# Routed expert layer with W1 as the stationary operand, fetched tile by tile

## The chip, the cores and the metric

One core of a Trainium2 chip runs the whole program. The metric is device microseconds of that core, median of several runs. The engines are PE (TensorE: matrix products, with PEld for its weight loads), DVE (VectorE), ACT (ScalarE), POOL (GpSimd) and SP (SyncE, which here only issues DMAs). A name with a q behind it, such as PEldq or SPq, is the sequencer of that engine. All data is float32.

## The reference, cut to what matters

The program applies four residual layers to 4096 tokens of width 256: linear attention, a routed expert layer, a state-space layer with a scan, and the expert layer once more with the same weights. Only the expert layer is touched:

```
logits = tokens @ Wr + br                    # tokens = layernorm(x), 4096 x 256, 8 experts
expert = argmax(softmax(logits)); max_prob = its probability
h = relu(tokens @ W1[expert] + b1[expert])   # W1: 8 x 256 x 512
y = h @ W2[expert] + b2[expert]              # W2: 8 x 512 x 256
x = x + y * max_prob
```

Each token goes through one expert only.

## The kernel before

The program is one `build` function with a section per engine; each engine executes its list in order, and semaphores (`wait_ge`, `then_inc`) join them. `feed(r)` is the expert layer, run for r = 0 (first stage below) and r = 1 (second stage). It normalises the rows, computes the logits, sorts tokens by expert and lays them into 39 tiles of 128 rows, each of one expert (`TILES = 39`). `tile_e` holds each tile's expert number, `idx` the row numbers. The semaphore `f_pos` says that `tile_e` is there, `f_idx` that `idx` is.

POOL gathers the rows of tile j into `t_x[j % 8]`, scatters the finished tile `t_y` to DRAM, and gathers tile j + 8. Even tiles use one set of buffers and PSUM banks, odd tiles the other (`par`). For each tile:

1. DVE `norm` (L917) writes the normalised rows `t_n`.
2. PE `tr` transposes them (2 transposes, L1108), ACT `xt` (L528) copies the result to `t_xt`.
3. PE `first` (L1261): the tokens are stationary, W1 of the tile's expert is moving, 512 columns wide; the result in `ps[2 + par]` has tokens on partitions.
4. DVE `hid` (L908) copies that to `t_h`.
5. PE `turn_hidden` transposes `t_h` in four 128 x 128 pieces (L1108) into `ps[4 + par]`.
6. ACT `relu` (L535, four instructions) adds b1, applies relu and writes `t_ht`.
7. PE `second` (L1278): `t_ht` is stationary, W2 is moving, 256 columns wide.
8. DVE `bias` (L927) and `result` (L934) make `t_y`.

A float32 product is executed as two passes, so `first` appears in the profile as 4 matmuls of 512 columns, `second` as 8 of 256 columns, and a transpose as one. All eight experts' W1 and W2 are in SBUF before a stage begins (`load_ffn`, 16 transfers of 512 KB and b2). PE reads the expert number from `tile_e` into a register (`expert`, L1253: a TENSOR_LOAD and some register instructions) right ahead of every `first` and every `second`. PE's order over a pair of tiles stands in the loop `turn`: turn_hidden(2i), first(2i+1), tr(2i+2), second(2i), turn_hidden(2i+1), first(2i+2), tr(2i+3), second(2i+1).

Of the kernel before, what the change touches and what calls it, by code (L numbers as in the profile page):

```python
# [17 lines left out]
P = 128  # L18
# [4 lines left out]
KD = D // P  # L23
# [63 lines left out]
AT_BANKS = ((6, 0, 3), (7, 3, 3), (1, 6, 2))  # L87


RING = 4  # L90


def h_buffers():
# [32 lines left out]
def build(nc, T):  # L126
    with ExitStack() as ctx:
# [52 lines left out]


        fs = Space(0)
        w1 = fs.take(E * KD * HID).rearrange("p (e k h) -> p e k h", e=E, k=KD)
        w2 = fs.take(E * KH * D).rearrange("p (e k d) -> p e k d", e=E, k=KH)
        b2 = fs.take(E * D).rearrange("p (e d) -> p e d", e=E)
        FEED = fs.at
# [41 lines left out]
        t_n = [s.take(D) for _ in range(2)]  # L228
        t_xt = [s.take(KD * P).rearrange("p (k t) -> p k t", k=KD) for _ in range(2)]
        assert s.at <= router + 4 * NCH * E, s.at  # L230
        s = Space(AR - 2 * KI * DI - KI * D - 5 * HID)
        t_h = [s.take(HID) for _ in range(2)]
        t_ht = [s.take(HID).rearrange("p (k t) -> p k t", k=KH) for _ in range(2)]
        t_y = [s.take(D) for _ in range(2)]
        s = Space(AR - 2 * KI * DI - KI * D)
# [49 lines left out]

        def load_ffn(eng, r):
            for e in range(E):
                eng.dma_start(w1[:, e], T["W1"][e].rearrange("(k p) h -> p k h", p=P)).then_inc(S(f"ld_ffn{r}"), 16)
                eng.dma_start(w2[:, e], T["W2"][e].rearrange("(k p) d -> p k d", p=P)).then_inc(S(f"ld_ffn{r}"), 16)
            eng.dma_start(b2, T["b2"].partition_broadcast(P)).then_inc(S(f"ld_ffn{r}"), 16)  # L290

        LD_FFN = 16 * (2 * E + 1)


        @block.sync
        def _(sp):
            xin = T["x"].rearrange("b (c p) d -> p b c d", p=P)
            for b in range(BATCH):
                if b == 1:
                    sp.dma_start(cst[:, :], T["cst"]).then_inc(S("ld_cst"), 16)  # L300
                sp.dma_start(x[:, b * CPB:(b + 1) * CPB, :], xin[:, b]).then_inc(S(f"ld_x{min(b, 1)}"), 16)
            sp.wait_ge(S("ld_x1"), 16 * (BATCH - 1))
            load_ffn(sp, 0)


            def store_rows(r, b):
                at = kept(b) if r else b * CPB
                sp.dma_start(xs[r][b * SEQ:(b + 1) * SEQ].rearrange("(c p) d -> p c d", p=P),
                             x[:, at:at + CPB, :]).then_inc(S(f"f{r}_rows"), 16)

            for b in range(BATCH):
                sp.wait_ge(S("a_xupd"), b + 1)
                store_rows(0, b)
            sp.wait_ge(S("row_zeroed"), 32)
            sp.dma_start(ipw, T["ip_x"].rearrange("(k p) d -> p k d", p=P)).then_inc(S("ld_ipw"), 16)
            for k in range(TAPS):
                if k >= 2:
                    sp.wait_ge(S("tap_mm"), KD * (k - 1))
                sp.dma_start(cw[k % 2], T["conv"][k].rearrange("(k p) d -> p k d", p=P)).then_inc(S(f"ld_cw{k}"), 16)

            sp.wait_ge(S("f0_st0"), 16 * (TURNS + 1))
            sp.wait_ge(S("f0_st1"), 16 * TURNS)
            for b in range(BATCH):
                sp.dma_start(x[:, b * CPB:(b + 1) * CPB, :],
                             x_mid[b * SEQ:(b + 1) * SEQ].rearrange("(c p) d -> p c d", p=P))\
                    .then_inc(S(f"ld_mid{min(b, 1)}"), 16)
            for b in range(BATCH):
                sp.wait_ge(S("m_bchi"), b + 1)
                sp.dma_start(c_rows[b % 2], m_bc[NS:2 * NS, :]).then_inc(S("m_cst"), 16)
                sp.wait_ge(S("m_cst"), 16 * (b + 1))  # L330
                for n in range(NS):
                    i = NS * b + n
                    if i >= RC:
                        sp.wait_ge(S("m_cp"), i - RC + 1)
                    if n == NS - 4 and b:
                        sp.wait_ge(S("m_xupd"), 2 * b)
                        store_rows(1, b - 1)
                    if n == 2 and 2 <= b < BATCH - 2:
                        new = b + RING - 2
                        sp.wait_ge(S("f1_rows"), 16 * (b - 1))  # L340
                        if b > 2:
                            sp.wait_ge(S("ld_again"), 16 * (b - 2))
                        sp.dma_start(x[:, kept(new):kept(new) + CPB, :],
                                     x_mid[new * SEQ:(new + 1) * SEQ].rearrange("(c p) d -> p c d", p=P))\
                            .then_inc(S("ld_again"), 16)
                    sp.dma_start(m_c[i % RC], c_rows[b % 2][n].partition_broadcast(P)).then_inc(S(f"m_cl{i % RC}"), 16)
            sp.wait_ge(S("m_y"), KI * BATCH)
            sp.wait_ge(S("f1_rows"), 16 * (BATCH - 1))
            sp.dma_start(x[:, RING * CPB:, :], xs[1][0:RING * SEQ].rearrange("(c p) d -> p c d", p=P))\
                .then_inc(S("ld_back"), 16)  # L350
            sp.wait_ge(S("m_xupd"), 2 * BATCH)
            store_rows(1, BATCH - 1)
            load_ffn(sp, 1)
            sp.wait_ge(S("f1_st0"), 16 * (TURNS + 1))
            sp.wait_ge(S("f1_st1"), 16 * TURNS)

# [81 lines left out]
        def _(a):  # L438
# [66 lines left out]
            def feed(r):  # L505
# [18 lines left out]

                def xt(par, n):
                    a.wait_ge(S(f"f{r}_tr{par}"), n + 1)
                    a.wait_ge(S(f"f{r}_h{par}"), n)
                    a.activation(t_xt[par], ps[par][:, 0:KD * P].rearrange("p (k t) -> p k t", k=KD), ACT.Copy)\  # L528
                        .then_inc(S(f"f{r}_xt{par}"), 1)

# [13 lines left out]
                a.wait_ge(S("f_pos"), r + 1)  # L544
                xt(0, 0)
                xt(1, 0)

                def turn(i, more):
                    relu(expert(2 * i), 0, i)
                    xt(0, i + 1)  # L550
                    relu(expert(2 * i + 1), 1, i)
                    if more:
                        xt(1, i + 1)

                turn(0, True)
                with a.Fori(1, H - 1) as i:
                    turn(i, True)
                turn(H - 1, False)
                relu(expert(TILES - 1), 0, H)

            feed(0)
            for k in range(TAPS // 2, TAPS):
# [113 lines left out]
        def _(v):  # L676
# [144 lines left out]
            def feed(r, updated, n_updated):  # L821
# [80 lines left out]
                v.tensor_copy(idx, r_col).then_inc(S("f_idx"), 1)  # L902
                link(v.tensor_copy(tabs, ps[4][:, 0:NV * COLS].rearrange("p (v j) -> p v j", v=NV)))

                def hid(par, n):
                    v.wait_ge(S(f"f{r}_h{par}"), n + 1)
                    v.wait_ge(S(f"f{r}_ht{par}"), n)
                    v.tensor_copy(t_h[par], ps[2 + par][:, :]).then_inc(S(f"f{r}_hc{par}"), 1)  # L908

                def norm(k, par):  # L910

                    j = 2 * k + par
# [24 lines left out]
                v.wait_ge(S(f"ld_ffn{r}"), LD_FFN)  # L937
                norm(0, 0)
                norm(0, 1)
                hid(0, 0)  # L940
                for k in range(TURNS):
                    norm(k + 1, 0)
                    hid(1, k)
                    bias(k, 0)
                    if k < TURNS - 1:
                        norm(k + 1, 1)
                    result(k, 0)
                    hid(0, k + 1)
                    bias(k, 1)
                    result(k, 1)  # L950
                bias(TURNS, 0)
# [153 lines left out]
        def _(t):  # L1105
# [104 lines left out]
            def feed(r):  # L1210
# [43 lines left out]
                                        min_val=0, max_val=E - 1)  # L1254

                def first(j, par, n):
                    e = expert(j)
                    t.wait_ge(S(f"f{r}_xt{par}"), n + 1)
                    t.wait_ge(S(f"f{r}_hc{par}"), n)
                    for k in range(KD):  # L1260
                        last = t.matmul(ps[2 + par][:, :], t_xt[par][:, k, :],  # L1261
                                        w1[:, row(e), k, :].rearrange("p a h -> p (a h)"),
                                        start=(k == 0), stop=(k == KD - 1))
                    last.then_inc(S(f"f{r}_h{par}"), 1)

                def turn_hidden(par, n):
                    t.wait_ge(S(f"f{r}_hc{par}"), n + 1)
                    t.wait_ge(S(f"f{r}_relu{par}"), n)
                    for k in range(KH):
                        last = turned(ps[4 + par][:, k * P:(k + 1) * P], t_h[par], k, 0)  # L1270
                    last.then_inc(S(f"f{r}_ht{par}"), 1)

                def second(j, par, n):
                    e = expert(j)
                    t.wait_ge(S(f"f{r}_relu{par}"), n + 1)
                    t.wait_ge(S(f"f{r}_y{par}"), n)
                    for k in range(KH):
# [9 lines left out]
                tr(1, 0)  # L1287
                first(0, 0, 0)

                def turn(i, more):  # L1290
                    turn_hidden(0, i)
                    first(2 * i + 1, 1, i)
                    tr(0, i + 1)
                    second(2 * i, 0, i)
                    turn_hidden(1, i)
                    first(2 * i + 2, 0, i + 1)
                    if more:
                        tr(1, i + 1)
                    second(2 * i + 1, 1, i)

                turn(0, True)
                with t.Fori(1, H - 1) as i:
                    turn(i, True)
                turn(H - 1, False)
                turn_hidden(0, H)
                second(TILES - 1, 0, H)

            def logits(r, b):
                t.wait_ge(S("f_xt"), BATCH * r + b + 1)
# [229 lines left out]
```

## Time and profile before

| | |
|---|---|
| median of 3 runs | 1665.94 us (1663.62 to 1668.23) |
| profiled execution | 1664.5 us, its span 1662.5 us |
| PE busy | 1431.1 us of the span |
| DVE, ACT, POOL busy | 1117.9, 951.9, 915.3 us |
| first expert stage, tiles 0 to 38 | about 293 to 466 us of the span |
| second expert stage, tiles 0 to 38 | about 1478 us to the end |

The busy shares are means over stages of different kinds; this change touches the two expert stages, some 350 us together. The span is 2.0 us shorter than the time of the same execution, and that time is 1.4 us under the median.

### The profile page before, as it was taken

The page shows a single profiled execution, that of the slowest core. Times are in us where ns is not written, and L with a number is a line of the kernel's source. Part 1 is how long each engine was busy: PE and PEld are TensorE (multiplying, and loading weights), DVE is VectorE, ACT ScalarE, POOL GpSimd, SP SyncE. Part 2 cuts the span into 40 slices and gives each one's busy share as a digit, 9 for nine tenths or more (in the row PEclk, how much of TensorE's full clock was granted, in tenths as well). Part 3 has the DMA queues.
Part 4 walks back from the last instruction along what each step waited for, and adds up shares of the span by engine and source line. Part 5 has one row for each costly group of instructions (what it writes and reads, how often), then busy time and mean ns, then how long its engine had stood idle before and what let it go on. Part 6 is the DMA issues. An engine that isn't in the chain of part 4 may idle for free.

```text
span 1662.5 us, 21266 instructions
## 1 busy us (share of the span) xinstructions
PE 1431.1 (86%) x6310; PEld 929.5 (56%) x6311; DVE 1117.9 (67%) x1703; ACT 951.9 (57%) x1749; POOL 915.3 (55%) x417
## 2 busy tenths in 40 slices
PE   2899877999998898989989999999996635779997
PEld 1566575566643555555655556555564524746664
DVE  5566546344451689999889998889999954354443
ACT  1222211333322899898998989999898840113332
POOL 1111000444300499979989898998989981024442
PEclk9999968999999899999999999999997875579999
DMA  9300021111130296894958949589494985211120
GB/s 311 131 25 25 26 76 54 58 61 59 44 102 14 50 221 138 186 202 114 219 129 200 215 115 219 132 194 212 108 220 111 211 182 198 92 30 60 59 60 17
DMA packets 81314, 202.87 MB, mean 122 GB/s; under 512 B 9609, under 2 KB 40462, under 8 KB 68688
## 3 DMA queue, kind: packets, MB, share of 16 engines
q0 software_dynamic: 21376, 119.30, 33.4%
q1 hardware_dynamic: 55632, 78.91, 14.9%
q10 hardware_dynamic: 4224, 3.67, 0.7%
q8 instruction: 38, 0.62, 0.1%
q14 instruction: 44, 0.36, 0.1%
HBM read 84.14 MB, written 18.88 MB: 62 GB/s over the span
## 4 chain that ended last, share of the span: by engine, by line
PE 63%; DVE 12%; ACT 10%; issue 8%; POOL 4%; DMA 2%; SPq 1%; ACTq 1%; POOLq 0%; DVEq 0%
PE ps L1108 13%; PE ps L1344 10%; PE ps L1278 9%; PE ps L1261 8%; DVE arena L1056 4%; PE ps L1373 4%; ACT arena L620 4%; ACT arena L630 3%; PE ps L1133 3%; PE ps L1313 3%; POOL arena L413 2%; PE ps L1415 2%; PE ps L1170 2%; PE ps L1124 2%; PE ps L1206 2%
## 5 line engine op out<-in xcount | busy, mean ns | idle before, releaser
L1108 PEld LDWEIGHTS ps<-cst,arena 128*128 128x128 f32 x2836 | 373.7, 151 | 407.6 <-issue 255.2
L1108 PE MATMUL ps<-cst,arena 128*128 128x128 f32 x2836 | 458.5, 291 | 113.4 <-ACT arena L630 48.4
L413 POOL TENSOR_TENSOR arena<-arena 128x2048 f32<-128x2048 f32 x98 | 460.3, 4699 | 119.0 <-DVE arena L1056 91.5
L1056 DVE TENSOR_TENSOR_SCAN arena<-arena,ps 128x512 f32<-128x512 f32 x392 | 471.2, 1212 | 62.1 <-PE ps L1108 54.6
L620 ACT ACTIVATE arena<-arena,a_neg 128x512 f32<-128x512 f32 x512 | 366.4, 716 | 50.7 <-DVE arena L1056 39.5
L630 ACT ACTIVATE arena<-arena,m_bt 128x512 f32<-128x512 f32 x512 | 363.3, 710 | 1.1 <-PE ps L1108 1.1
L1344 PE MATMUL ps<-arena,tapw 128*128 128x512 f32 x512 | 260.4, 608 | 0.0
L382 POOL DMA_INDIRECT arena<-rows,arena x78 | 75.7, 970 | 250.0 <-DVE arena L902 226.5
L535 ACT ACTIVATE arena<-ps,b1t 128x128 f32<-128x128 f32 x312 | 89.0, 368 | 168.5 <-PE ps L1108 110.2
L1278 PE MATMUL ps<-arena 128*128 x624 | 151.3, 385 | 6.6 <-ACT arena L535 3.2
L1056 DVE TENSOR_TENSOR_SCAN x<-arena,ps 128x512 f32<-128x512 f32 x120 | 143.9, 1211 | 18.6 <-PE ps L1108 16.5
L1261 PE MATMUL ps<-arena 128*128 x312 | 152.4, 612 | 0.8 <-issue 0.8
L413 POOL TENSOR_TENSOR x<-x,arena 128x2048 f32<-128x2048 f32 x30 | 140.1, 4670 | 5.7 <-DMA arena<-c_rows 4.2
L1373 PE MATMUL ps<-arena,dtw 128*128 128x512 f32 x256 | 130.7, 598 | 2.2 <-ACT arena L585 1.2
L1278 PEld LDWEIGHTS ps<-arena 128*128 128x128 f32 x624 | 112.3, 190 | 28.6 <-issue 16.5
L927 DVE TENSOR_TENSOR arena<-ps,arena 128x256 f32<-128x256 f32 x78 | 33.2, 425 | 123.3 <-PE ps L1278 71.0
L1415 PE MATMUL ps<-outw,arena 128*128 128x256 f32 x256 | 74.3, 407 | 37.6 <-DVE arena L1016 37.6
L908 DVE COPY arena<-ps 128x512 f32<-128x512 f32 x78 | 54.0, 692 | 78.2 <-PE ps L1261 78.2
L1344 PEld LDWEIGHTS ps<-arena,tapw 128*128 128x128 f32 x512 | 85.0, 195 | 29.5 <-issue 28.4
L373 POOL TENSOR_TENSOR x<-x,arena 128x1024 f32 (+1 forms) x8 | 18.8, 2350 | 132.0 <-DVE arena L711 126.7
L396 POOL DMA_INDIRECT out_x<-arena x39 | 39.5, 1013 | 92.1 <-DVE arena L934 92.1
L528 ACT ACTIVATE arena<-ps 128x256 f32<-128x256 f32 x78 | 29.9, 384 | 104.5 <-PE ps L1108 87.1
(152 smaller groups left out, 1668.6 us busy)
## 6 DMA issues: line engine op xcount, KB each, us to landing
arena<-arena POOLq DMA_DIRECT2D x45, 1024.0 KB, 8.8
arena<-c_rows SPq DMA_DIRECT2D x128, 256.0 KB, 3.8
x<-arena POOLq DMA_DIRECT2D x29, 1024.0 KB, 8.4
arena<-in_W SPq DMA_DIRECT2D x32, 512.0 KB, 10.2
arena<-x POOLq DMA_DIRECT2D x15, 1024.0 KB, 9.0
rows<-x SPq DMA_DIRECT2D x16, 512.0 KB, 3.3
x<-x POOLq DMA_DIRECT2D x7, 1024.0 KB, 8.9
x<-residual SPq DMA_DIRECT2D x12, 512.0 KB, 5.5
```

The source lines that it names most:

```text
L382: g.indirect_dma_start(out=t_x[j % XB], out_offset=None, in_=xs[r], in_offset=bass.IndirectOffsetOnAxis(ap=idx[:, j:j + 1], axis=0))\
L413: g.tensor_tensor(h, h, m_c[i % RC].unsqueeze(1).to_broadcast([P, KI, SEQ]), ALU.mult)\
L535: last = a.activation(t_ht[par][:, k, :], ps[4 + par][:, k * P:(k + 1) * P], ACT.Relu, bias=b1t[:, row(e), k:k + 1].rearrange("p a b -> p ...
L620: a.activation(m_a[g % RA], m_dt[b % 2][:, k, :], ACT.Exp, scale=a_neg[:, k, n:n + 1])\
L630: a.activation(m_dbt[i % 2][:, c, :], m_wt[b % 2][:, c, :], ACT.Copy, bias=1e-6, scale=m_bt[b % 2][:, c, n:n + 1]).then_inc(S("m_dbt"), 1)
L1056: v.tensor_tensor_scan(out=h[:, k, :], data0=m_a[g % RA], data1=ps[SCAN_BANK[g % 3]][:, :], initial=0.0, op0=ALU.mult, op1=ALU.add).then_i ...
L1108: return t.transpose(bank, src[:, k * P:(k + 1) * P], ident)
L1261: last = t.matmul(ps[2 + par][:, :], t_xt[par][:, k, :], w1[:, row(e), k, :].rearrange("p a h -> p (a h)"), start=(k == 0), stop=(k == KD ...
L1278: last = t.matmul(ps[6 + par][:, 0:D], t_ht[par][:, k, :], w2[:, row(e), k, :].rearrange("p a h -> p (a h)"), start=(k == 0), stop=(k == K ...
L1344: mm = t.matmul(ps[CONV_BANK[o]][:, :], tapw[:, k, d, o * P:(o + 1) * P], m_xt[n % 2][:, d, k:k + SEQ], start=(i == 0), stop=(i == TAPS * ...
L1373: mm = t.matmul(ps[DT_BANK[o]][:, :], dtw[:, k, o * P:(o + 1) * P], m_u[n % 2][:, k, :], start=(k == 0), stop=(k == KI - 1))
L1415: mm = t.matmul(ps[OUT_BANK[h]][:, (c % 2) * D:(c % 2) * D + D], m_sz[:, k, c * P:(c + 1) * P], outw[:, k, :], start=(k == 0), stop=(k == ...
```

## The change

W1 becomes the stationary operand of the first product. For each quarter h of the 512 hidden units, the product of W1's 128 x 128 block and the transposed tokens gives the hidden layer already transposed, in `ps[4 + par]`. So `hid` on DVE and `turn_hidden` on PE go, with their buffers. A tile's W1 (512 KB) is no longer resident: SP reads the tile's expert number, waits until the buffer's last reader, tile j - 4, is through its first product, and issues one DMA into `t_w1[j % 4]`. PE's `first` needs no register then, gets a wait for its W1 buffer and one for the relu of the tile that used its PSUM bank before; `second` gets its expert number from a read placed ahead of the `first` before it. PE's loop is written out. ACT's `relu` of an even tile stands at the end of a turn instead of the start of the next, which keeps ACT's order of work the same.

```diff
-RING = 4
+RING, WR = 4, 4
...
-        w1 = fs.take(E * KD * HID).rearrange("p (e k h) -> p e k h", e=E, k=KD)
+        t_w1 = [fs.take(KD * HID).rearrange("p (k h) -> p k h", k=KD) for _ in range(WR)]
...
             for e in range(E):
-                eng.dma_start(w1[:, e], T["W1"][e].rearrange("(k p) h -> p k h", p=P)).then_inc(S(f"ld_ffn{r}"), 16)
                 eng.dma_start(w2[:, e], T["W2"][e].rearrange("(k p) d -> p k d", p=P)).then_inc(S(f"ld_ffn{r}"), 16)
...
+            def send_w1(r):
+
+                sp.wait_ge(S("f_pos"), r + 1)
+                for j in range(TILES):
+                    if j >= WR:
+                        sp.wait_ge(S(f"f{r}_ht{j % 2}"), (j - WR) // 2 + 1)
+                    e = sp.value_load(tile_e[0:1, j:j + 1], min_val=0, max_val=E - 1)
+                    sp.dma_start(t_w1[j % WR], T["W1"][ds(e, 1)].rearrange("a (k p) h -> p (a k) h", p=P))\
+                        .then_inc(S(f"f{r}_w{j % WR}"), 16)
...
-                def hid(par, n):
-                    v.wait_ge(S(f"f{r}_h{par}"), n + 1)
-                    v.wait_ge(S(f"f{r}_ht{par}"), n)
-                    v.tensor_copy(t_h[par], ps[2 + par][:, :]).then_inc(S(f"f{r}_hc{par}"), 1)
...
                 def first(j, par, n):
-                    e = expert(j)
+
                     t.wait_ge(S(f"f{r}_xt{par}"), n + 1)
-                    t.wait_ge(S(f"f{r}_hc{par}"), n)
-                    for k in range(KD):
-                        last = t.matmul(ps[2 + par][:, :], t_xt[par][:, k, :],
-                                        w1[:, row(e), k, :].rearrange("p a h -> p (a h)"),
-                                        start=(k == 0), stop=(k == KD - 1))
-                    last.then_inc(S(f"f{r}_h{par}"), 1)
-
-                def turn_hidden(par, n):
-                    t.wait_ge(S(f"f{r}_hc{par}"), n + 1)
                     t.wait_ge(S(f"f{r}_relu{par}"), n)
-                    for k in range(KH):
-                        last = turned(ps[4 + par][:, k * P:(k + 1) * P], t_h[par], k, 0)
+                    t.wait_ge(S(f"f{r}_w{j % WR}"), 16 * (j // WR + 1))
+                    for h in range(KH):
+                        for k in range(KD):
+                            last = t.matmul(ps[4 + par][:, h * P:(h + 1) * P], t_w1[j % WR][:, k, h * P:(h + 1) * P],
+                                            t_xt[par][:, k, :], start=(k == 0), stop=(k == KD - 1))
                     last.then_inc(S(f"f{r}_ht{par}"), 1)
...
-                def turn(i, more):
-                    turn_hidden(0, i)
+                for i in range(H):
+                    even = expert(2 * i)
                     first(2 * i + 1, 1, i)
                     tr(0, i + 1)
-                    second(2 * i, 0, i)
-                    turn_hidden(1, i)
+                    second(even, 0, i)
+                    odd = expert(2 * i + 1)
                     first(2 * i + 2, 0, i + 1)
-                    if more:
+                    if i < H - 1:
                         tr(1, i + 1)
-                    second(2 * i + 1, 1, i)
...
-                turn_hidden(0, H)
-                second(TILES - 1, 0, H)
+                second(expert(TILES - 1), 0, H)
```

This is PE's order before, inside the loop of the first stage, for one even tile: the hidden turn, the first product of the next tile, the token turn, and the second product (L1108 is either kind of transpose, ISA a register instruction).

```order
L1108 MATMUL ps<-cst,arena 128x128 [waits f0_relu0,f0_hc0]
L1108 MATMUL ps<-cst,arena 128x128 x3
L1253 ISA
L1253 TENSOR_LOAD tile_e
L1253 ISA x2
L1261 ISA [waits f0_hc1,f0_xt1]
L1261 MATMUL ps<-arena 128x512
L1261 ISA
L1261 MATMUL ps<-arena 128x512
L1245 REGISTER_ALU
L1108 MATMUL ps<-cst,arena 128x128 [waits f0_xt0,f0_n0]
L1108 MATMUL ps<-cst,arena 128x128
```

Behind these stood a second TENSOR_LOAD and the second product. Now the same place reads as follows, with L1265 the first product, L1110 the token turn and L1274 the second product.

```order
L1255 TENSOR_LOAD tile_e
L1255 ISA x2
L1265 MATMUL ps<-arena 128x128 [waits f0_w3,f0_relu1,f0_xt1]
L1265 MATMUL ps<-arena 128x128 x7
L1110 MATMUL ps<-cst,arena 128x128 [waits f0_xt0,f0_n0]
L1110 MATMUL ps<-cst,arena 128x128
L1274 ISA [waits f0_y0,f0_relu0]
L1274 MATMUL ps<-arena 128x256
```

The four hidden transposes are gone, eight narrow products stand for two wide ones, one register read is left, and nothing but the second product's own register instructions stands between the token turn and it.

SP had nothing to do during the tiles: its queue went from the tap weights straight to the residual, as here.

```order
L319 DMA arena<-in_conv 128x4x512 [waits tap_mm] x2
L324 DMA x<-residual 128x4x256 [waits f0_st1,f0_st0]
L324 DMA x<-residual 128x4x256 x7
L329 DMA c_rows<-arena 16x512 [waits m_bchi]
L346 DMA arena<-c_rows 128x512 [waits m_cst]
```

Between the first two of these rows now stand 39 groups of the kind shown next; this is SP's queue around the fifth tile.

```order
L316 DMA arena<-in_W 128x2x512
L315 TENSOR_LOAD tile_e [waits f0_ht0]
L315 ISA x2
L316 ISA
L316 DMA arena<-in_W 128x2x512
```

From the fifth tile on, each transfer of W1 is released by the first product four tiles back.

## Rows read from the trace of the kernel before

**Rows 1.** Window, first expert stage: PE, PEld, DVE, ACT, POOL, clock, DMA, GB/s
```profile
303.00:453.00 150.00, 148.33 (x634) 100.15 (x633) 65.83 (x140) 53.37 (x175) 65.58 (x66) 1.00 0.18 54
```

**Rows 2.** Chain, one tile of the second stage: start, duration, work
```profile
1499.43 0.44 PE ps L1108 x4
1499.87 1.72 PE ps L1261 x4
1501.81 1.73 PE ps L1278 x8
```

**Rows 3.** Chain, both ends of the second stage
```profile
1475.60 2.73 DMA arena<-rows,arena
...
1479.68 3.79 PE ps L1261 x4
1483.50 0.70 DVE arena L908
...
1489.15 1.73 PE ps L1278 x8
...
1647.23 1.73 PE ps L1278 x8
...
1650.83 2.00 PE ps L1278 x8
```

**Rows 4.** Chain, both ends of the first stage
```profile
294.23 3.64 PE ps L1261 x4
...
301.71 1.73 PE ps L1278 x8
...
459.65 1.73 PE ps L1278 x8
...
463.54 1.99 PE ps L1278 x8
```

**Rows 5.** Timeline of PE's weight loads around one token turn
```profile
1496.55 0.14 PEld L1108 LDWEIGHTS ps<-cst,arena 128*128 128x128 f32 x1 [0.24 <-DVE arena L917]
...
1497.44 1.59 PEld L1278 LDWEIGHTS ps<-arena 128*128 128x128 f32 x8 [0.32 <-issue]
```

**Rows 6.** Timeline of PE, the row behind the second product ahead of that turn
```profile
1494.82 0.60 PE L1108 MATMUL ps<-cst,arena 128*128 128x128 f32 x4
```

**Rows 7.** Timeline of DVE in the same stretch
```profile
1495.14 0.42 DVE L927 TENSOR_TENSOR arena<-ps,arena 128x256 f32<-128x256 f32 x1 [1.38 <-PE ps L1278]
...
1496.01 0.41 DVE L917 TENSOR_SCALAR arena<-arena 128x256 f32<-128x256 f32 x1
```

**Rows 8.** Line L1253, PE's read of the expert number: ns min/median/max
```profile
L1253 PEldq TENSOR_LOAD <-tile_e x156: 296/302/495, 293.2 to 1648.0; - x156
```

**Rows 9.** Chain in the attention stage: eight transposes, sixteen passes of 129 columns
```profile
152.30 0.87 PE ps L1108 x8
153.17 1.79 PE ps L1154 x16
```

**Rows 10.** Chain in the logits: sixteen passes of 8 columns
```profile
229.63 3.21 PE ps L1313 x16
```

**Rows 11.** Window over the logits; the third last number is the granted clock
```profile
228.00:256.00 28.00, 28.00 (x136) 28.00 (x134) 4.14 (x12) 5.43 (x10) 0.00 (x0) 0.50 0.00 1
```

**Rows 12.** Timeline of ACT, one relu of a tile
```profile
1495.55 1.15 ACT L535 ACTIVATE arena<-ps,b1t 128x128 f32<-128x128 f32 x4 [1.88 <-issue]
```

**Rows 13.** Timeline of POOL: scatter of one tile, gather of another
```profile
1496.94 1.02 POOL L396 DMA_INDIRECT out_x<-arena  x1 [1.56 <-DVE arena L934]
1498.26 0.97 POOL L382 DMA_INDIRECT arena<-rows,arena  x1 [0.30 <-issue]
```

**Rows 14.** DMA issues, 1384 to 1415 us: KB each, median us to landing
```profile
arena<-in_W SPq DMA_DIRECT2D x16, 512.0 KB, 9.9
...
rows<-x SPq DMA_DIRECT2D x1, 512.0 KB, 3.3
```

**Rows 15.** Timeline of DVE where tile_e is written, second stage
```profile
1471.41 0.18 DVE L899 TENSOR_SCALAR tile_e<-arena 128x40 int32<-128x40 f32 x1
```

More of the change, by code:

```diff
@@ L230, in build @@
         assert s.at <= router + 4 * NCH * E, s.at
-        s = Space(AR - 2 * KI * DI - KI * D - 5 * HID)
-        t_h = [s.take(HID) for _ in range(2)]
+        s = Space(AR - 2 * KI * DI - KI * D - 3 * HID)
         t_ht = [s.take(HID).rearrange("p (k t) -> p k t", k=KH) for _ in range(2)]
@@ L287, in load_ffn @@
             for e in range(E):
-                eng.dma_start(w1[:, e], T["W1"][e].rearrange("(k p) h -> p k h", p=P)).then_inc(S(f"ld_ffn{r}"), 16)
                 eng.dma_start(w2[:, e], T["W2"][e].rearrange("(k p) d -> p k d", p=P)).then_inc(S(f"ld_ffn{r}"), 16)
             eng.dma_start(b2, T["b2"].partition_broadcast(P)).then_inc(S(f"ld_ffn{r}"), 16)
-        LD_FFN = 16 * (2 * E + 1)
+        LD_FFN = 16 * (E + 1)
         @block.sync
@@ L319, in _ @@
                 sp.dma_start(cw[k % 2], T["conv"][k].rearrange("(k p) d -> p k d", p=P)).then_inc(S(f"ld_cw{k}"), 16)
+            send_w1(0)
             sp.wait_ge(S("f0_st0"), 16 * (TURNS + 1))
@@ L353, in _ @@
             load_ffn(sp, 1)
+            send_w1(1)
             sp.wait_ge(S("f1_st0"), 16 * (TURNS + 1))
@@ L526, in xt @@
                     a.wait_ge(S(f"f{r}_tr{par}"), n + 1)
-                    a.wait_ge(S(f"f{r}_h{par}"), n)
+                    a.wait_ge(S(f"f{r}_ht{par}"), n)
                     a.activation(t_xt[par], ps[par][:, 0:KD * P].rearrange("p (k t) -> p k t", k=KD), ACT.Copy)\
@@ L546, in feed @@
                 xt(1, 0)
+                relu(expert(0), 0, 0)
                 def turn(i, more):
-                    relu(expert(2 * i), 0, i)
                     xt(0, i + 1)
@@ L553, in turn @@
                         xt(1, i + 1)
+                    relu(expert(2 * i + 2), 0, i + 1)
                 turn(0, True)
@@ L558, in feed @@
                 turn(H - 1, False)
-                relu(expert(TILES - 1), 0, H)
             feed(0)
@@ L939, in feed @@
                 norm(0, 1)
-                hid(0, 0)
                 for k in range(TURNS):
                     norm(k + 1, 0)
-                    hid(1, k)
                     bias(k, 0)
@@ L947, in feed @@
                     result(k, 0)
-                    hid(0, k + 1)
                     bias(k, 1)
@@ L1256, in first, with second @@
                 def first(j, par, n):
-                    e = expert(j)
                     t.wait_ge(S(f"f{r}_xt{par}"), n + 1)
-                    t.wait_ge(S(f"f{r}_hc{par}"), n)
-                    for k in range(KD):
-                        last = t.matmul(ps[2 + par][:, :], t_xt[par][:, k, :],
-                                        w1[:, row(e), k, :].rearrange("p a h -> p (a h)"),
-                                        start=(k == 0), stop=(k == KD - 1))
-                    last.then_inc(S(f"f{r}_h{par}"), 1)
-                def turn_hidden(par, n):
-                    t.wait_ge(S(f"f{r}_hc{par}"), n + 1)
-                    t.wait_ge(S(f"f{r}_relu{par}"), n)
-                    for k in range(KH):
-                        last = turned(ps[4 + par][:, k * P:(k + 1) * P], t_h[par], k, 0)
+                    t.wait_ge(S(f"f{r}_relu{par}"), n)
+                    t.wait_ge(S(f"f{r}_w{j % WR}"), 16 * (j // WR + 1))
[3 more added lines that the diff above has]
+                                            t_xt[par][:, k, :], start=(k == 0), stop=(k == KD - 1))
                     last.then_inc(S(f"f{r}_ht{par}"), 1)
-                def second(j, par, n):
-                    e = expert(j)
+                def second(e, par, n):
                     t.wait_ge(S(f"f{r}_relu{par}"), n + 1)
@@ L1288, in feed @@
                 first(0, 0, 0)
-                def turn(i, more):
-                    turn_hidden(0, i)
+                for i in range(H):
+                    even = expert(2 * i)
                     first(2 * i + 1, 1, i)
                     tr(0, i + 1)
-                    second(2 * i, 0, i)
-                    turn_hidden(1, i)
+                    second(even, 0, i)
+                    odd = expert(2 * i + 1)
                     first(2 * i + 2, 0, i + 1)
-                    if more:
+                    if i < H - 1:
                         tr(1, i + 1)
-                    second(2 * i + 1, 1, i)
[L1301 to L1304, printed above, removed]
-                turn_hidden(0, H)
-                second(TILES - 1, 0, H)
+                    second(odd, 1, i)
+                second(expert(TILES - 1), 0, H)
             def logits(r, b):
```

## The prediction

> **What bounds the kernel now.** I read three views for the two expert stages: windows, the chain, then the timelines. In a window of 150 us inside the first stage PE is busy for 148 us at the full granted clock, while DVE, ACT and POOL have 66, 53 and 66 us of work [rows 1]. So PE's own list sets the pace there. The chain agrees, in both stages alike: a tile is a hidden turn of 0.44 us, a first product of 1.72 and a second of 1.73, all PE [rows 2]; the token turn, half a hidden turn, is 0.22. These make 4.11 us. From the second product of tile 0 to that of tile 37, 37 tiles on, the second stage takes 1647.23 - 1489.15 = 158.08 us, or 4.27 a tile [rows 3], and the first 157.94, the same 4.27 [rows 4]. The missing 0.16 is in one place of each pair of tiles. DVE ends a norm at 1496.01 + 0.41 = 1496.42 [rows 7], the token turn's load is released by it, and the loads of the second product start only at 1497.44, after 0.32 us without work [rows 5]. In that 1.02 us PE's sequencer, which had stood at the norm's semaphore, reads the expert number (0.30 us for the TENSOR_LOAD alone [rows 8]) and works out addresses. Everywhere else the read is hidden, because the sequencer runs ahead of the array.
>
> **The steady tile after the change.** Removed: the hidden turn, 0.44 us of PE, and DVE's copy. DVE is not the bound, so the copy counts only where it stood in the way of something.
>
> Exchanged: 4 passes of 512 columns for 16 passes of 128. The columns are the same, 2048, but there are 16 weight loads of 128 x 128 instead of 4, so what matters is whether a load fits behind 128 moving columns. The nearest row is the key/value product of the attention stage, a stationary 128 x 128 from SBUF with 129 columns moving: 16 passes in 1.79 us, and 8 transposes in 0.87 [rows 9]. These give 1.78 and 1.74 us for 16 passes. The load alone is seen where almost nothing moves: 16 passes of 8 columns take 3.21 us, 0.20 each [rows 10], but at half the clock [rows 11], so 0.10 at the full one, against 0.107 for the columns. It fits, barely. I take 1.75 for the first product, 0.03 more than now.
>
> A rule speaks against this. The Trainium skill, "TensorE: Matmul & The Clock Gate", section "Back-to-back issue gap", says that in a real stream the spacing is set by the load and the product together, about 81 ns at 128 columns where the product alone would need 56. By that ratio, as an estimate from the page, the first product would take about 2.5 us and the kernel would lose. The row of 129 columns in float32 does not show such an addition, and the sum goes by the row.
>
> Moved: the register read. It now stands ahead of the first product, where the sequencer is some 1.2 us ahead of the array (it has passed a second product of 1.73 us within about half a microsecond, at one register instruction per product). The read and its register work cost about 0.65 of that, my estimate: the 1.02 us less what the semaphore, the turn's dispatch and the first load need. So the gap of 1.02 us behind a norm shrinks to about 0.35, nearly covered by the turn itself. This returns most of the 0.16 a tile.
>
> New on the same place: the norm is late next. The second product ahead of a norm hands over at 1494.82 [rows 6]; DVE's bias, result and norm follow and end at 1496.42 [rows 7], 1.60 us later, with no copy between them in the old order either. PE needs 0.05 us to see it and 0.1 for the load, so the turn can start at 1.75. Before, a hidden turn and a first product (2.16) covered this; now a first product of 1.75 alone does. I expect a wait of 0 to 0.3 us per pair of tiles, for the norms of even tiles only (the other norm stands ahead of the result in DVE's list), and take 0.15, the middle.
>
> A tile: 1.75 + 0.22 + 1.73 + 0.075 = 3.775 us. Against 4.27 that is 0.495 less; times 37, 18.3 a stage, 36.6 in both.
>
> **The other engines at this pace.** ACT must bring the relu between the end of a first product and the second product of the same tile, which are a first product and a turn of other tiles apart, 1.97 us, plus a second product. It takes 1.15 [rows 12], some 0.3 to hear of PE, and the wait for the copy ahead of it: free by over a microsecond. POOL needs from a result to the end of the next gather 0.9 to start (from DVE's next operation at 1496.01 [rows 7] to 1496.94), 1.02, 0.30 and 0.97, together 3.2 us [rows 13], less than 3.775 by 0.6. SP, idle until now, waits, reads and issues once a tile, about 1.2 us by my estimate, 0.65 for the read and half a microsecond for the issue. Behind its waits stand only later W1 transfers and, after the last, the load of the residual, which waits for the last scatter anyway.
>
> W1's transfer: a buffer is freed at the end of a first product and needed four tiles on, 4 x 3.775 - 1.75 = 13.3 us later. SP takes 1.2 of these; a 512 KB transfer lands 3.3 us after issue alone and 9.9 in a queue of seventeen [rows 14]. In this stage at most one or two are in flight, 0.5 MB in 3.775 us beside 55 GB/s of rows [rows 1], so I take 4 to 6 us. Cost 0; it starts to cost above 12 us. The transfers of a dynamic address on SP are not in the trace; below, a static issue bounds them, above, the queue of seventeen.
>
> **The ends of a stage.** Start: from the first product of tile 0 to the second product of tile 0 the second stage took 9.47 us [rows 3], the first 7.48 [rows 4], at half the clock for most of it; in it stand a copy of 0.70 us on DVE [rows 3] and a hidden turn, 0.88 at half the clock, with nothing else for PE to do. These go. The clock may rise later relative to the work, since the work comes sooner. I take 1.5 a stage (bounds 0.5 and 2.8). Against it stands that the first four W1 transfers, 2 MB, now run beside the first gathers, of which the first takes 2.73 us to land and is on the chain [rows 3]. `tile_e` is written at 1471.6 [rows 15], 8 us ahead of the first product, so W1 of tile 0 is there in time; the gathers may land later. I take 0.5 a stage (0 to 2).
>
> End: from the end of tile 37's second product to the start of tile 38's passed 1650.83 - 1648.96 = 1.87 us in the second stage and 463.54 - 461.38 = 2.16 in the first [rows 3, 4], for a hidden turn and a relu that nothing covered. Now tile 38's relu runs beside the second product of tile 37. Gain 4.0 together.
>
> Less W1 in `load_ffn` frees 4 MB of early transfers; the work that follows them waits for other things, so 0.
>
> **Sum.** 36.6 + 3.0 - 1.0 + 4.0 = 42.6 us. From the profiled execution's 1664.5, 1621.9; it was 1.4 under the median of the runs, so 1622 to 1623. I say 1622.
>
> **Rivals.**
> *The load shows.* If half of each 0.10 us load stood outside the columns, the first product would take 16 x 0.157 = 2.5 us, a tile 4.53, and the kernel 74 x 0.26 - 6 = 13 us more: 1679. With the whole load outside, 16 x 0.207 = 3.3, a tile 5.3, 1739. It decides from 0.145 us a pass on. The page named above says something like the first. Against it: 0.111 a pass measured [rows 9]. Chance 3 in 100.
> *The clock falls.* In the logits PE is busy throughout, with passes of 8 columns and transposes, and is granted half the clock [rows 11]. If that came with the new stage's passes too, a tile would take 3.7 us more, and 11 such tiles of 78 would use up the gain. Against it: the logits move 8 columns where these move 128 and 256, the array is filled as before, and transposes are fewer. Chance 2; a fourth of the tiles so: 1694.
> *W1 comes late.* Should a transfer need over 15.6 us from a free buffer to landing, a tile takes over (15.6 + 1.75) / 4 = 4.35 us and the kernel is slower; at 18 us, 4.9 a tile, 1709. Only a queue of seventeen came near that. Chance 2.
> *A partial wait.* W1's traffic or the tighter round of DVE and POOL costs something on every tile, through late norms, gathers or scatters, and the tile takes 3.9 to 4.1: 74 x 0.27 + 6 = 26 us gained at 4.0, 1640. POOL's slack of 0.6 and the norm's of nothing speak for it. Chance 13.
> *It does nothing,* because the sequencer can't cover the read and the waits with 16 loads to issue: PE stays at 4.27. Chance 2.
> *The forecast,* 78. Its own range: tiles of 3.70 to 3.87 (43 or 30 us), ends between 10 and 3 us, so 1613 to 1633.
>
> **Numbers.** The range reaches into the partial wait: 1612 to 1636. A difference under 0.3% (5 us) can't be told from none. Faster: forecast, partial wait and a bit, 92; same 2; slower 6.
>
> **What would show it.** Right: 16 passes at L1265 in 1.75 us, no gap over 0.1 us behind the token turn, 3.7 to 3.8 us between second products, SP's W1 landing within 6 us, PE waiting nowhere for a W1 semaphore, the clock at 1.00. Wrong: loads of L1265 that leave gaps, a token turn that waits for DVE L917 by more than 0.3 us per pair, PE idle released by a DMA into arena, late first gathers, a clock under 1 between tiles 3 and 38.

## The result, and the profile after

| | before | after |
|---|---|---|
| median of 4 runs | 1664.78 us (1663.61 to 1668.23) | 1615.16 us (1611.79 to 1626.81) |
| ratio after / before | | 0.9722, interval 0.9695 to 0.9749 |
| span of the profiled execution | 1662.5 us | 1615.4 us |

The profiled execution of the changed kernel took 1617.17 us, 2.0 over the median. PE's share and the groups that answer to the changed lines, from the page of the changed kernel:

```profile
PE 1385.1 (86%) x6934; PEld 979.2 (61%) x6934; DVE 1063.7 (66%) x1625; ACT 952.1 (59%) x1749; POOL 916.6 (57%) x417
L1265 PE MATMUL ps<-arena 128*128 128x128 f32 x1248 | 155.8, 280 | 0.0
L1274 PE MATMUL ps<-arena 128*128 x624 | 147.4, 380 | 0.0
```

A window inside each stage (busy us of PE, PEld, DVE, ACT, POOL; clock; DMA share; GB/s), to be held against [rows 1]:

```profile
303.00:433.00 130.00, 130.00 (x908) 122.75 (x907) 41.60 (x105) 53.01 (x174) 65.23 (x66) 1.00 0.66 197
1470.00:1590.00 120.00, 120.00 (x839) 113.40 (x838) 38.54 (x98) 48.94 (x161) 62.60 (x63) 1.00 0.68 208
```

PE has no idle time left at the full clock; the DMA engines now carry 200 GB/s instead of 54, and DVE has 42 us of work in 130. The chain, for one tile and both ends of the first stage, answers to [rows 2] and [rows 4]:

```profile
283.92 5.13 DMA arena<-rows,arena
289.74 0.66 PE ps L1110 x2
290.40 1.53 issue
291.93 0.69 PE ps L1110 x2
292.62 5.20 PE ps L1265 x32
298.03 1.73 PE ps L1274 x8
299.76 1.78 PE ps L1265 x16
301.55 0.22 PE ps L1110 x2
301.76 1.73 PE ps L1274 x8
...
436.08 3.57 PE ps L1274 x16
439.64 13.78 PE ps L1208 x32
```

A tile is 1.78 + 0.22 + 1.73 = 3.73 us with no gap. The second products of tiles 37 and 38 stand as one piece of 16 passes at 436.08: the wait of 2.16 us at the end of the stage is gone. The second stage, also from the chain:

```profile
1448.89 5.11 DMA arena<-rows,arena
...
1455.35 2.04 issue
1457.39 0.69 PE ps L1110 x2
1458.07 6.11 PE ps L1265 x32
...
1464.40 1.73 PE ps L1274 x8
...
1602.26 1.74 PE ps L1274 x8
```

At both starts the gather of tile 0 takes 5.1 us to land. What PE waits for last is the gather of tile 1, for both token turns stand ahead of the first product in PE's list. The 2.73 us of [rows 3] is that gather too: POOL issues it behind the gather of tile 0. These are its issue and the norm that it releases, in the first stage of the changed kernel:

```profile
285.27 0.97 POOL L392 DMA_INDIRECT arena<-rows,arena  x1 [0.30 <-issue]
291.40 0.47 DVE L922 TENSOR_SCALAR arena<-arena 128x256 f32<-128x256 f32 x1 [1.81 <-DMA arena<-rows,arena]
```

From issue to norm pass 6.13 us, and 6.66 in the second stage; before it was 2.76 in both. The token turn of tile 1 so comes 2.2 and 2.7 us behind that of tile 0.

Split by pieces of the two spans:

| piece | before | after | difference |
|---|---|---|---|
| 37 tiles, first stage | 157.94 | 138.05 | -19.9 |
| 37 tiles, second stage | 158.08 | 137.86 | -20.2 |
| from tile 37's second product to PE's next work (L1208) | 5.88 | 3.56 | -2.3 |
| the same to the end of the span, second stage | 15.27 | 13.14 | -2.1 |
| start of each stage, from the cast of `idx` to the second product of tile 0 | 14.02, 15.77 | 15.00, 16.35 | +1.0, +0.6 |
| everything else (attention, logits, sort, scan) | | | -4.1 |

The last line can't be laid to the change. Of it, 2.8 us are in the first logits, which are the same code. From the first to the last record of the logits product passed 33.45 and 36.56 us in the two stages of the kernel before, 30.62 and 36.55 after. The granted clock was 1.00 for the first 3.4 us of the 33.45 and for the first 6.5 us of the 30.62, then 0.50; in both stretches of 36.6 it was 0.50 from the start. In all profiles of this study, of whichever kernel, the stretch is near one of 30.6, 33.5 and 36.6. Another 1.4 us are ahead of the first logits, which begin at 222.5 us before and 221.1 after; in the thirteen profiles they begin between 218.3 and 222.7, with no order by kernel.

### The profile page after: what moved, and what is told of

It reads as the page before. It is cut to its first block, busy times and chain, and to the rows that moved or that the text cites. A ratio compares the mean times of both kernels' runs of the same rounds, so it can differ in the third digit from the quotient of the medians.

```text
span 1615.4 us, 22069 instructions
## 1 busy us (share of the span) xinstructions
PE 1385.1 (86%) x6934; PEld 979.2 (61%) x6934; DVE 1063.7 (66%) x1625; ACT 952.1 (59%) x1749; POOL 916.6 (57%) x417
## 4 chain that ended last, share of the span: by engine, by line
PE 62%; ACT 11%; DVE 11%; issue 8%; POOL 4%; DMA 2%; SPq 1%; ACTq 1%; POOLq 0%; DVEq 0%
PE ps L1110 11%; PE ps L1334 10%; PE ps L1265 9%; PE ps L1274 8%; ACT arena L630 4%; ACT arena L640 4%; PE ps L1363 4%; DVE arena L1058 4%; PE ps L1135 3%; PE ps L1303 3%; POOL arena L423 2%; PE ps L1405 2%; PE ps L1172 2%; PE ps L1126 2%; PE ps L1208 2%
## 5 line engine op out<-in xcount | busy, mean ns | idle before, releaser
L1110 PEld LDWEIGHTS ps<-cst,arena 128*128 128x128 f32 x2524 | 330.8, 152 | 364.0 <-issue 234.2
L1110 PE MATMUL ps<-cst,arena 128*128 128x128 f32 x2524 | 410.2, 293 | 119.4 <-ACT arena L640 49.3
L392 POOL DMA_INDIRECT arena<-rows,arena x78 | 76.0, 974 | 246.0 <-DVE arena L912 222.5
L1265 PEld LDWEIGHTS ps<-arena 128*128 128x128 f32 x1248 | 155.6, 197 | 3.8
L1265 PE MATMUL ps<-arena 128*128 128x128 f32 x1248 | 155.8, 280 | 0.0
L1274 PE MATMUL ps<-arena 128*128 x624 | 147.4, 380 | 0.0
L1274 PEld LDWEIGHTS ps<-arena 128*128 128x128 f32 x624 | 112.5, 190 | 12.4 <-issue 0.2
L521 ACT ACTIVATE arena<-ps 128x512 f32<-128x512 f32 x32 | 17.4, 594 | 113.4 <-PE ps L1110 113.4
```

The lines of the kernel that those rows point to most:

```text
L392: g.indirect_dma_start(out=t_x[j % XB], out_offset=None, in_=xs[r], in_offset=bass.IndirectOffsetOnAxis(ap=idx[:, j:j + 1], axis=0))\
L1110: return t.transpose(bank, src[:, k * P:(k + 1) * P], ident)
L1265: last = t.matmul(ps[4 + par][:, h * P:(h + 1) * P], t_w1[j % WR][:, k, h * P:(h + 1) * P], t_xt[par][:, k, :], start=(k == 0), stop=(k == ...
L1274: last = t.matmul(ps[6 + par][:, 0:D], t_ht[par][:, k, :], w2[:, row(e), k, :].rearrange("p a h -> p (a h)"), start=(k == 0), stop=(k == K ...
```

## The experiments

In all of them "a tile" is the mean over 36 tiles, from the start of tile 0's second product to tile 36's, first and second stage, and "the start" is the stretch from the cast of `idx` to tile 0's second product. On this scale the kernel before has 4.277 and 4.281, the changed kernel 3.737 and 3.732. Ratios are to the kernel before as timed beside each experiment: its median was 1664.69 us beside the three on the read and the first hold, 1663.61 beside the later ones on the hold, and 1662.72 beside the others.

### The register read alone

```diff
-                def first(j, par, n):
-                    e = expert(j)
+                def first(e, par, n):
...
-                def second(j, par, n):
-                    e = expert(j)
+                def second(e, par, n):
...
+                    nums[1] = expert(2 * i + 1)
+                    first(nums[1], 1, i)
...
-                    second(2 * i, 0, i)
+                    second(nums[0], 0, i)
```

> The kernel before, with PE's register read alone changed: each tile's expert number is read once, ahead of its first product, and kept for its second. Theory (the read behind the norm's semaphore makes the gap of each pair): a tile falls from 4.27 to 4.11 to 4.14 us, the kernel by 10 to 12 us, to about 1654. Rival (the gap is the norm's lateness or the loop's branch, and the read hides anyway): 4.27 a tile, 1665.

Measured: 1649.33 us, ratio 0.9916 (0.9896 to 0.9935), a tile 4.103 in both stages. The timeline of PE's weight loads, as in [rows 5]:

```profile
384.71 0.14 PEld L1108 LDWEIGHTS ps<-cst,arena 128*128 128x128 f32 x1 [0.24 <-DVE arena L917]
385.14 0.14 PEld L1108 LDWEIGHTS ps<-cst,arena 128*128 128x128 f32 x1 [0.29 <-issue]
385.25 1.60 PEld L1276 LDWEIGHTS ps<-arena 128*128 128x128 f32 x8
```

The turn's first load is released by the norm as before, and the second product's loads now follow without idle time. 74 tiles by 0.176 is 13 us of the 15.4 between the medians; the rest was not followed up. This edit includes the written-out loop, so that was run by itself too:

```diff
-                turn(0, True)
-                with t.Fori(1, H - 1) as i:
-                    turn(i, True)
-                turn(H - 1, False)
+                for i in range(H):
+                    turn(i, i < H - 1)
```

> The kernel before with PE's loop over the tiles written out and nothing else. Theory: the branch stands where the sequencer is ahead, so 4.27 us a tile as before, 1663 to 1668. Rival: the branch or the reading of instructions costs something, and the tile changes by over 0.03 us.

Measured: 1659.67 us in one run, 4.219 and 4.255 a tile. So up to 0.06 of the 0.176 is the loop and not the place of the read; it is not quite nothing, as I had thought. In the first stage the chain still has 0.24 us of the gap per pair: every other second product takes 1.97 us there in place of 1.73. In a loop the number's address takes a register instruction ahead of the TENSOR_LOAD, on the same late path; that this is the cause was not tested apart.

### The read put back

```diff
-                    even = expert(2 * i)
                     first(2 * i + 1, 1, i)
                     tr(0, i + 1)
-                    second(even, 0, i)
-                    odd = expert(2 * i + 1)
+                    second(expert(2 * i), 0, i)
```

> The changed kernel with PE's read put back right ahead of the second product. Theory: at the turns of even tiles the sequencer stands at the norm's semaphore until 1.64 us after the second product before, then needs the 1.02 us of the kernel before up to the first load: 2.66 instead of 1.89, 0.77 us per pair, 0.39 a tile, so 4.11 us a tile and 28 us more, about 1643. Rival (the read hides once the hidden turn is gone): 3.73 a tile, 1615.

Measured: 1639.09 us, ratio 0.986 (0.9841 to 0.9879), a tile 4.093 and 4.097. The chain has the gap where it was foretold, behind one token turn of two:

```profile
381.74 1.78 PE ps L1265 x16
383.53 0.22 PE ps L1110 x2
383.75 0.35 issue
384.10 1.99 PE ps L1274 x8
386.09 1.78 PE ps L1265 x16
387.87 0.22 PE ps L1110 x2
```

The other turn, whose norm is early, has none. A pair is 0.72 us longer than in the changed kernel, of which the chain shows 0.35 as idle and 0.26 in the second product behind it, 1.99 in place of 1.73. So without the early read the change would have gained about half. The two parts don't add: the read costs 0.12 to 0.18 a tile in the kernel before and 0.36 here. The numbers fit the hidden turn having covered part of the norm's lateness: 0.35 a pair before, plus the 0.38 by which hidden turn and first product (2.16) were longer than the first product alone (1.78), gives 0.73. This was not tested by itself.

### W1 without the stream

```diff
-        t_w1 = [fs.take(KD * HID).rearrange("p (k h) -> p k h", k=KD) for _ in range(WR)]
+        w1 = fs.take(E * KD * HID).rearrange("p (e k h) -> p e k h", e=E, k=KD)
...
-                            last = t.matmul(ps[4 + par][:, h * P:(h + 1) * P], t_w1[j % WR][:, k, h * P:(h + 1) * P],
+                            last = t.matmul(ps[4 + par][:, h * P:(h + 1) * P], w1[:, j % E, k, h * P:(h + 1) * P],
```

> The changed kernel with all eight W1 resident again and no transfers during the tiles; tile j uses the W1 of expert j mod 8 whatever its own number, so the routing of the first product is left out and the rest is as in the changed kernel. Theory (the stream of W1 costs nothing in the steady tiles and only delays the first gathers): 3.73 us a tile, and from the idx cast to the second product of tile 0 11.5 to 13 us instead of 15.2 and 16.5, so 5 to 8 us faster than the changed kernel. Rival (the stream also costs on steady tiles): under 3.70 a tile.

Measured: 1606.23 us, ratio 0.9679 (0.9632 to 0.9725), a tile 3.733 and 3.732, starts of 11.75 and 12.21. The window inside the first stage:

```profile
303.00:433.00 130.00, 130.00 (x906) 122.76 (x906) 41.10 (x104) 53.50 (x175) 65.66 (x66) 1.00 0.21 64
```

With 64 GB/s or with 197, a tile takes the same. The stream costs nothing on steady tiles and 3.3 plus 4.1 us at the two starts. The gather of tile 1 is 2.8 and 2.9 us from its norm again. Against the changed kernel the time is 8.9 us less by the medians and 7 by the ratios, where 5 to 8 was expected.

### The stream held back at the start

```diff
                 for j in range(TILES):
+                    if j == 2:
+                        sp.wait_ge(S("f_x1"), 16 * (r * ((TILES - 1 + XB - 1) // XB) + 1))
                     if j >= WR:
```

> The changed kernel with W1 of tiles 2 and 3 (and all later ones) held back on SP until the gather of tile 1 has landed. Theory (the four early W1 transfers make the first gathers late): the stretch from the cast that makes idx to the second product of tile 0 falls from 15.2 and 16.5 us to 12 to 13.5, the kernel by 4 to 7 us. Half only if the transfers of tiles 0 and 1 do half of the harm. Rival (the gathers are late for another cause, such as POOL itself): the stretch stays at 15 and 16.5.

Measured: 1615.03 us, ratio 0.969 (0.9669 to 0.9711), a tile 3.733 and 3.734, starts of 12.57 and 13.52. The stretch behaved as the theory said, and the median did not move against the changed kernel's 1615.16. The chain at the first start:

```profile
287.91 4.68 DMA arena<-rows,arena
...
293.28 1.08 PE ps L1112 x4
294.36 0.10 issue
294.46 4.91 PE ps L1267 x32
```

The first gather still takes 4.68 us, since W1 of tiles 0 and 1 run beside it; but the second lands with it, and both turns stand in one piece, where the changed kernel had 1.5 us between them. From the issue of tile 1's gather to its norm pass 3.8 and 3.6 us in the two stages, in place of 6.1 and 6.7. Both kernels were timed again side by side.

> The changed kernel once more, as the yardstick for the two runs beside it on the same chip: 1611 to 1619, starts of 15 and 16.5 us (idx cast to the second product of tile 0), 3.73 a tile.

> W1 of tiles 2 and up held back until the gather of tile 1 has landed, timed beside the changed kernel. In its first profile the starts were 12.6 and 13.5 us instead of 15.0 and 16.4. Theory: these 5 us show in the time as well, 1606 to 1614. Rival: the untouched parts, whose length differs by several us from run to run, drown it, and the two can't be told apart.

Measured: the changed kernel 1614.28 us (1612.15 to 1619.12, six runs; starts 15.78 and 15.62), the held one 1610.60 (1609.23 to 1616.55, six runs; starts 12.58 and 12.92), ratios to the kernel before 0.9719 (0.9693 to 0.9745) and 0.9698 (0.9672 to 0.9725). The medians differ by 3.7 us in the expected direction, of the 5 expected; the single runs and the intervals overlap. The gain is shown by the stretch itself, in four starts, and only suggested by the whole time.

The hold one tile earlier (`if j == 1`):

> The same with the hold one tile earlier: W1 of tile 1 too waits for the gather of tile 1. Theory: the first gathers are as quick as without the stream (2.7 us), but W1 of tile 1 lands 4.7 us after the gather of tile 1, while its first product is wanted about 4.5 us after it at half the clock, so the start is within 0.5 us of 12.6 and 13.5. Rival: if the transfer of tile 1 did harm by itself, the start falls below 12 us.

Measured: 1610.96 us in one run, starts of 13.67 and 14.31, about 1.2 us longer than with the hold at tile 2. Neither side had this. The gathers are as quick as without the stream, 2.8 us to the norm of tile 1, and the first product of tile 0 starts earlier, but from there to tile 0's second product it takes 7.5 and 8.2 us, where the hold at tile 2 had 5.0 to 6.2. In the first stage little of this is a wait for W1 of tile 1: PE idles 0.20 us ahead of tile 1's first product, at 297.17 us, but ACT's relu of tile 0 begins only at 299.49, 2.5 us after the last record of tile 0's first product, and the second product waits for it. What held the relu is not shown. In the second stage PE idles 0.69 us and the relu is 1.2 us behind. In this one profile, holding at tile 2 is the better place of the two.

### How long a W1 transfer takes

The change is `WR = 2` and `WR = 1` in place of 4, with SP's wait on the parity of tile j - WR.

> Two buffers of W1 instead of four. The packets of the changed kernel show a transfer landing 3.6 to 4.9 us after its issue starts; with the semaphore and SP's read about 5.0 to 6.2 from a free buffer. A tile can't be shorter than (that + 1.78) / 2 = 3.4 to 4.0 us. Theory: 3.73 to 3.95 a tile, with waits of PE for W1 on some tiles, 0 to 15 us more. Rival (a landing of 9 us, as the median over all W transfers on the page reads): 5.4 a tile, over 120 us more.

> One buffer of W1, so that each transfer waits for the first product of the tile before and the next first product for the transfer: the tile shows the whole way from a free buffer to landing. Theory: 5.0 to 6.2 plus 1.78 gives 6.8 to 8.0 us a tile, the kernel 230 to 315 us slower. Rival (9 us to landing): over 11 us a tile, over 530 us slower.

Measured: two buffers 1616.97 us in one run, 3.809 and 3.810 a tile; one buffer 1870.30, 7.033 and 6.963 a tile. The chain with one buffer shows the whole way:

```profile
382.06 2.04 PE ps L1265 x16
384.10 0.02 issue
384.11 0.27 SPq L315
...
384.82 3.87 DMA arena<-in_W
388.69 0.14 issue
388.82 3.52 PE ps L1265 x16
```

SP hears of the freed buffer at once, reads the number and issues in 0.7 us; the transfer lands 3.87 later, and PE starts 0.14 behind it: 4.7 us from freed to used. (The 3.52 is a product at a granted clock of 0.55; over 310 to 430 us the mean clock is 0.91, with PE busy for 77 of 120 us.) With two buffers the bound is (4.7 + 1.78) / 2 = 3.24, so the transfer is hidden but for single late ones, 0.08 a tile. Four buffers, 4 x 3.73 - 1.78 = 13.1 us of time for 4.7, are more than the kernel needs. Two buffers also let only two transfers run beside the first gathers, and the starts were 14.24 and 13.45 us, shorter than the changed kernel's: a further sign that the early transfers are what makes them long.

### The pace of the weight loads

```diff
-                            last = t.matmul(ps[4 + par][:, h * P:(h + 1) * P], t_w1[j % WR][:, k, h * P:(h + 1) * P],
-                                            t_xt[par][:, k, :], start=(k == 0), stop=(k == KD - 1))
+                            last = t.matmul(ps[4 + par][:, h * P:h * P + 32], t_w1[j % WR][:, k, h * P:(h + 1) * P],
+                                            t_xt[par][:, k, 0:32], start=(k == 0), stop=(k == KD - 1))
```

> The first product moves only 32 of the 128 tokens through each stationary block of W1; the hidden layer of the other 96 tokens is left out, so only the pace of the weight loads is of interest. If the load needs 0.10 us, as half of the logits' 0.20 at half the clock says, the 16 passes take 1.6 us instead of 1.78, at the full clock, and the load is hidden by less than 0.01 us a pass. If the load were much shorter the passes would follow the columns, 0.03 us each, 0.5 us in all. The tile then may not get shorter by as much, since the norm of even tiles is there only 1.64 us after the second product before.

Measured: the chain has

```profile
380.36 1.71 PE ps L1265 x16
382.06 0.25 PE ps L1110 x2
382.31 1.73 PE ps L1274 x8
384.04 1.70 PE ps L1265 x16
```

16 passes take 1.70 to 1.71 us with a quarter of the columns, 0.106 to 0.107 a pass, not 0.10. So this is a pace at the full clock that the columns don't set. I take it for that of the loads; a limit on issue was not tested apart, but one that ignores the array's clock doesn't fit, since at half the clock a pass took 0.20 [rows 10]. The first product at 1.78 is only 4% above it: the load is hidden, with nothing to spare. A row of the kernel before would have told me directly, had I looked at the first logits, where the clock is still high; this is its chain:

```profile
222.67 1.69 PE ps L1313 x16
224.35 0.93 PE ps L1108 x8
225.28 2.55 PE ps L1313 x16
```

The stage as a whole was not shorter but longer, 3.773 and 3.854 a tile (1619.41 us in one run). There the chain runs at times through a scatter and DVE's bias, which waits for it before it may overwrite `t_y`:

```profile
392.59 0.74 issue
393.33 6.21 DMA residual<-arena
...
399.75 0.44 DVE arena L932
```

6.2 us from issue to landing beside the stream is 1.6 tiles of time. In this run it is a late scatter that stops DVE, and then PE, at some tiles.

## Why the prediction was right

The time is inside the range, and the steady tile came out by the mechanism that was forecast. That the sum came out so near is in part luck, as the starts below show.

- **PE's own list bounds the stage, and the columns decide.** Right. With the stream and without it, a tile is exactly the sum of PE's passes.
- **The first product at 1.75 us.** Measured 1.78, the value of the 129 column row. Of the rival that the load shows, this leaves 0.07 us: 1.78 against 1.71 for the loads and 1.72 for the same columns in four passes. The Trainium skill's 81 against 56 ns ("TensorE: Matmul & The Clock Gate", "Back-to-back issue gap"), taken as a ratio for float32 passes, does not agree with this trace: 1.78 against 1.72 us.
- **The read moved ahead returns most of the 0.16 a tile.** Right, by the experiment on the kernel before: 0.176 with the written-out loop, at least 0.12 without it.
- **The norm late next, 0.15 us a pair.** Wrong in size: there is no wait. The norm's path is 1.75 us as reckoned, the first product that must cover it is 1.78 and not 1.75, and the turn's load starts inside its last pass. The 0.075 a tile less for the wait and the 0.03 more for the first product are what the tile beat the forecast by, 3.73 for 3.775. That the margin is thin was right: with the read behind the norm a pair was 0.72 us longer, where 0.77 was expected.
- **Transfers hidden.** Right; for 4 to 6 us from issue to landing the medians in the first stage are 3.7 us with one buffer and 4.0 with two. For the changed kernel itself the profile tells no landings in the steady tiles.
- **Start of a stage, net gain 2.0 in both.** Wrong in sign: net loss 1.6. It has two parts. From the first product of tile 0 to its second product the gain was 2.07 and 3.14 us, more than the 3.0 together that I took. From the cast to the first product the loss was 3.0 and 3.7, where I took 0.5 a stage with a bound of 2. The mechanism, gathers beside 2 MB of W1, was the one named, and the hold and the run without a stream both show it. The term was mis-sized twice over. The row of 2.73 us was read as the gather of tile 0, but it is that of tile 1, on which the first product waits and which is hit harder: 6.1 and 6.7 us to its norm in place of 2.8. And the time that 2 MB takes was not worked out: the queue of seventeen moved some 360 GB/s, which gives 5.8 us, and in the changed kernel the DMA engines moved 334 GB/s between 284 and 288 us, while the first gathers were under way.
- **End of a stage, 4.0.** Measured 4.4.

The terms together gave 42.6 and the pieces of the two stages measure 43.0: 40.1 + 4.4 - 1.6. Two errors, 3.5 too little on the tiles and 3.6 too much on the starts, cancelled by luck. The remaining distance between 1622 and 1615.16 is not the change's: 4.1 us are the untouched parts in the two profiled executions, and 2.0 are the changed kernel's profiled execution above its median. So of the 49.6 us between the medians about 43 are shown to come from the change.

## What to carry to other kernels

Look for what an engine's sequencer does behind a late semaphore, not only for what the engine does: a register read of 0.3 us cost nothing where the sequencer ran ahead, and 0.24 to 0.35 us each time before and 0.72 in the changed kernel where it stood behind a late wait, and the cure is to place it ahead of the wait. If a product's result must be transposed anyway, see whether the operands can change roles; here float32 passes of 128 columns took 1.78 us where passes of 512 took 1.72, and the transposes and the copy go. A stream of weights that was free in the steady state cost 3 to 4 us at each start, where it met the small transfers that everything waits for: send first what is waited for, and hold the rest.

## What the runs showed of the hardware that was not expected

- 16 float32 passes, each with its load of 128 x 128, took 1.69 to 1.71 us at the full clock whether 8 or 32 columns moved; at half the clock, 8 columns, 3.21 us, which is less than twice as much.
- In the logits the granted clock was 0.50 from the first product on in some executions, and in others fell to 0.50 after 3.4 or 6.5 us at 1.00, while PE was busy throughout; this alone moves the logits, which are on the chain, by steps of 3 us. In the run with 32 moving columns, between products of 256 columns, it stayed at 1.00 and 0.98.
- A gather of 128 rows landed 2.7 us after issue without the stream; beside the first four transfers of 512 KB the first gather took 5.1 us and the second 6 to 6.7 up to its norm. In the steady tiles with two buffers the medians are 3.8 us for a gather and 4.5 for a scatter, where they were 2.8 and 2.5 with one buffer and half the traffic.
